# Attention with batch 1's value stage inside batch 0's value products, and whole fp32 operands for the first half of the queries

## The reference

```
V = x @ wv.T + bv                       # then out @ wo.T + bo: both fold into one 256 x 256 matrix here
pos = x @ w3d.T + b3d                   # three coordinates per token
dist = pairwise_l2(pos)
scores = where(causal, -inf, -dist[:, None] * scale)     # the same for all 16 heads
attn = softmax(scores)
x = x + attn @ V (projected)            # layer 1
x = x + experts(layernorm(x))           # layer 2: router, shared and routed experts
```

## Time and profile before

| What | Time, us |
|---|---|
| median of three runs | 684.58 |
| the profiled execution | 679.88 |
| its span | 678.1 |
| TensorE busy | 573.9 (85%) |
| VectorE busy | 449.8 (66%) |
| ScalarE busy | 339.8 (50%) |
| GpSimd busy | 211.7 (31%) |
| batch 0: first distance, first value product, last product's start | 62.01, 91.33, 142.21 |
| batch 1: first transpose, first distance, first value product, last product's start | 146.45, 188.05, 217.37, 268.25 |
| first TensorE work of the second layer | 277.94 |
| four tiles normalised on VectorE (L364) | 1.37 |
| two low parts of a transposed group (L370) | 1.28 |
| ScalarE's table load; exponential, high part of a block of 512 columns | 1.28; 0.62; 0.64 |

### The profile page before, as it was taken

One profiled execution on the slowest core, in us unless ns is written; L12 is line 12 of the kernel. 1 busy time (PEld: TensorE's weight loads), 2 busy tenths in 40 slices (PEclk: granted clock), 3 DMA queues, 4 the chain that ended last, 5 costly groups with the idle time before them and its releaser, 6 DMA issues.

```text
span 678.1 us, 11259 instructions
## 1 busy us (share of the span) xinstructions
PE 573.9 (85%) x3484; PEld 501.0 (74%) x3484; DVE 449.8 (66%) x1143; ACT 339.8 (50%) x710; POOL 211.7 (31%) x404
## 2 busy tenths in 40 slices
PE   3738989977498998684299899899999999998995
PEld 2727789977477998453278777688888888887884
DVE  4983898978578974878777776344444444444985
ACT  0416977614388781461454554255555555553331
POOL 2061120012323000000566777155455455452000
PEclk9978579979675999697599999899999999999998
DMA  9988000000000000920122222233333333325941
GB/s 283 313 246 3 1 1 1 2 0 1 1 0 1 2 1 1 347 118 1 55 79 87 91 91 86 79 102 102 109 105 102 106 103 106 104 79 177 383 161 62
DMA packets 57127, 62.59 MB, mean 92 GB/s; under 512 B 14736, under 2 KB 50448, under 8 KB 57072
## 3 DMA queue, kind: packets, MB, share of 16 engines
q1 hardware_dynamic: 49216, 43.46, 22.7%
q0 software_dynamic: 6480, 17.77, 7.3%
q10 hardware_dynamic: 1376, 0.66, 0.4%
HBM read 30.50 MB, written 31.37 MB: 91 GB/s over the span
## 4 chain that ended last, share of the span: by engine, by line
PE 42%; DVE 11%; ACT 4%; issue 3%; POOL 0%; DVEq 0%; ACTq 0%; POOLq 0%
PE bank L1208 12%; PE bank L1209 11%; PE bank L1210 11%; PE bank L1329 2%; PE bank L1345 2%; PE bank L1217 1%; DVE hf L1138 1%; ACT W_hi L911 1%; ACT h_hi L891 1%; DVE XN L974 1%; DVE XR L974 1%; DVE X L1129 1%; DVE XT_lo L1019 1%; DVE W_lo L1153 1%; DVE sw_lo L1027 1%
## 5 line engine op out<-in xcount | busy, mean ns | idle before, releaser
L843 POOL DMA_INDIRECT token_out<-YS,to_row x71 | 69.6, 980 | 96.1 <-ACT YS L941 92.5
L827 POOL DMA_INDIRECT slots_in<-XR,slot x64 | 69.8, 1091 | 82.5 <-DVE XR L1108 67.2
L575 PE MATMUL a_bank<-VO,E_hi 128*128 128x258 f32 x272 | 78.7, 289 | 4.3 <-DVE E_lo L482 4.3
L579 PE MATMUL a_bank<-VO,E_lo 128*128 128x258 f32 x272 | 78.1, 287 | 0.0
L577 PE MATMUL a_bank<-VO,E_hi 128*128 128x256 f32 x272 | 78.1, 287 | 0.0
L1179 DVE TENSOR_TENSOR hr<-bank,sr 128x256 f32<-128x256 f32 x71 | 30.1, 424 | 61.9 <-ACT sr L929 61.9
L453 DVE TENSOR_SCALAR E<-a_bank 128x512 f32<-128x512 f32 (+3 forms) x80 | 45.9, 606 | 29.3 <-PE a_bank L565 29.3
L1208 PE MATMUL bank<-W_hi,XST_hi 128*128 x142 | 62.4, 440 | 0.5 <-DVE XST_lo L1183 0.5
L1208 PE MATMUL bank<-XT_hi,sw_hi 128*128 128x512 f32 x128 | 52.4, 410 | 10.0 <-DVE XT_lo L1019 8.4
L929 ACT ACTIVATE sr<-bank 128x256 f32<-128x256 f32 x71 | 27.4, 385 | 64.1 <-PE bank L1210 64.1
L1210 PE MATMUL bank<-W_hi,XST_lo 128*128 x142 | 56.8, 400 | 0.0
(11 more groups left out here) (227 smaller groups left out, 1650.5 us busy)
## 6 DMA issues: line engine op xcount, KB each, us to landing
XS<-slots_in SPq DMA_DIRECT2D x71, 129.0 KB, 2.0
YG<-token_out SPq DMA_DIRECT2D x16, 512.0 KB, 7.8
slots_in<-blank SPq DMA_DIRECT2D x7, 1161.0 KB, 14.7
W_raw<-in_wT_dram SPq DMA_DIRECT2D x8, 768.0 KB, 12.6
X<-in_x_dram SPq DMA_DIRECT2D x8, 512.0 KB, 7.2
out_dram<-X SPq DMA_DIRECT2D x32, 128.0 KB, 2.1
token_out<-YS,to_row POOLq DMA_INDIRECT x71, 2.4
slots_in<-blank SPq DMA_DIRECT2D x1, 1032.0 KB, 13.7
```

Source lines behind the costliest of these rows:

```text
L575: pe.matmul(O_ps[Q % 2][j][:, 0:D + 2], E_hi[:, n % NE, cols], VO[:, kt, 0:D + 2], start=(kt == 0), stop=False)
L579: mm = pe.matmul(O_ps[Q % 2][j][:, 0:D + 2], E_lo[:, n % NE, cols], VO[:, kt, 0:D + 2], start=False, stop=(kt == qt))
L827: pool.indirect_dma_start(out=xs, out_offset=bass.IndirectOffsetOnAxis(ap=slot[k][:, t:t + 1], axis=0), in_=XR[:, t % 4, k, :], in_offset= ...
L843: pool.indirect_dma_start(out=ys, out_offset=bass.IndirectOffsetOnAxis(ap=to_row[:, i:i + 1], axis=0), in_=YS[:, i % NYS, :], in_offset=No ...
```

## The change

- **Whole operands in the first half.** Blocks 0 to 11 are no longer split. `VO` holds whole fp32 values and one column of ones (257 columns), and a tile pair is one fp32 product (L661 of the changed kernel). `VS` holds the values' high and low parts for the second half (L663 to L667).
- **The values are split on GpSimd** (L282, L284), per key tile behind its two selects.
- **Distances and products are interleaved.** 18 blocks of distances come first, then two more before each product until block 40 is reached.
- **Batch 1's stages 1 and 2 stand inside batch 0's products,** from product 17 on (`SIDE`), on all engines: group transposes, value tiles in pairs, maximum, features, feature transposes at products 34 to 36.
- Query groups share one set of four output banks; the other four serve distances and batch 1's value stage. `E_hi` and `E_lo` have four slots and lie where the first half's `E` was. In the second half ScalarE makes all high parts, VectorE the low ones two blocks ahead.
- All of batch 1's statistics run before batch 0's distances, and its root of the variance before batch 0's roots.

```diff
-VW = 2 * D + 2
+VW = D + 1
+HW = 2 * D + 2
-NE = 8
+NE = 4
-        O_ps = (bank[0:4], bank[4:8])
+        O_ps = bank[4:8]
+        N_FIRST = blocks.index((halves[1][0], 0))
+        EARLY = N_FIRST + 6
+        SIDE = 17
+        AHEAD = 2
+        def scores_before(n):
+
+            return range(min(EARLY + 2 * n, NBLK), min(EARLY + 2 * n + 2, NBLK))
...
@@ gpsimd, behind the two selects of key tile kt
+                    pool.wait_ge(s_voh, b * TB + kt + 1)
+                    pool.tensor_copy(VS[:, kt, 0:D], VO[:, kt, 0:D]).then_inc(s_vh, 1)
+                    pool.wait_ge(s_vh, b * TB + kt + 1)
+                    pool.tensor_tensor(VS[:, kt, D + 2:HW], VO[:, kt, 0:D], VS[:, kt, 0:D].bitcast(f32),
+                                       ALU.subtract).then_inc(s_vl, 1)
...
@@ scalar
+                roots(b, halves[0])
+                act.wait_ge(s_dist, b * NROW + GT * halves[0][-1] + GT)
+                for n in range(N_FIRST):
+                    exponential(b, n)
+                roots(b, halves[1])
+                act.wait_ge(s_dist, (b + 1) * NROW)
+                for n in range(N_FIRST, N_FIRST + 2 * AHEAD):
+                    exponential(b, n)
+                for n in range(N_FIRST, N_FIRST + AHEAD):
+                    high_part(b, n)
+                for n in range(N_FIRST, NBLK):
+                    if n + 2 * AHEAD < NBLK:
+                        exponential(b, n + 2 * AHEAD)
+                    if n + AHEAD < NBLK:
+                        high_part(b, n + AHEAD)
+                    if b + 1 < NB and n >= SIDE:
+                        next_values(b + 1, n - SIDE)
...
@@ vector
+            def next_values(b, m):
+                if m == 0:
+                    reciprocal_std(b)
+                if m % 2 == 0 and m // 2 < GB:
+                    normalise(b, m // 2)
+                if m % 2 == 1 and m // 2 < GB:
+                    group_lo(b, m // 2)
+                if 3 <= m < 3 + 2 * GB:
+                    for j in range(2):
+                        positions(b, (m - 3) // 2, (m - 3) % 2 * 2 + j)
+                if m == 2 * GB + 3:
+                    features(b)
...
+                for n, (Q, kt) in enumerate(blocks):
+                    for m in scores_before(n):
+                        square(b, m)
+                    if n == N_FIRST - 1:
+                        for m in range(N_FIRST, N_FIRST + AHEAD):
+                            split_lo(b, m)
+                    if N_FIRST <= n < NBLK - AHEAD:
+                        split_lo(b, n + AHEAD)
+                    if b + 1 < NB and n >= SIDE:
+                        next_values(b + 1, n - SIDE)
+                    if kt >= GT * Q:
+                        finish(b, Q, kt - GT * Q)
...
@@ tensor
+                    if whole:
+                        mm = pe.matmul(O_ps[j][:, 0:VW], blk[:, cols], VO[:, kt, :], start=(kt == 0), stop=(kt == qt))
...
+                for n in range(EARLY):
+                    distances(b, n)
+                for n in range(NBLK):
+                    for m in scores_before(n):
+                        distances(b, m)
+                    value_products(b, n)
+                    if b + 1 < NB and n >= SIDE:
+                        next_values(b + 1, n - SIDE)
```

More of the change, by code:

```diff
@@ L12 @@
 MW = D + 4
-VW = 2 * D + 2
-TRI = sum(S - P * k for k in range(TB))
+VW = D + 1
+HW = 2 * D + 2
 KR = 32
@@ new lines, in roots, with exponential @@
+            def roots(b, half):
+                for kt in range(GT * half[-1] + GT):
+                    row = row_of(half, kt)
+                    act.wait_ge(s_e2, b * NBLK + sq_blocks.index((half[-1], kt)) + 1 + NQ)
+                    act.wait_ge(s_diag, 2 * (b * TB + kt) + 2)
+                    act.activation(row, row, ACT.Sqrt).then_inc(s_dist, 1)
+            def exponential(b, n):
+                blk = block_of(*blocks[n])[0]
+                act.activation(blk, blk, ACT.Exp, scale=-SCALE).then_inc(s_exp, 1)
@@ new lines, in high_part @@
+            def high_part(b, n):
+                blk, _, w = block_of(*blocks[n])
+                act.wait_ge(s_exp, b * NBLK + n + 1)
+                act.wait_ge(s_eb, b * NBLK + free_for(n, HI_FREE) + 1)
+                act.activation(E_hi[:, n % NE, 0:w], blk, ACT.Copy).then_inc(s_eh, 1)
+            deviations(0)
+            group_hi(0, 0)
+            for g in range(GB):
+                if g + 1 < GB:
+                    group_hi(0, g + 1)
+                for j in range(GT):
+                    values(0, g, j)
@@ new lines, in _ @@
+            for n in range(3 * GB):
+                features(0, n)
+            for b in range(NB):
+                if b + 1 < NB:
+                    deviations(b + 1)
+                roots(b, halves[0])
[15 more added lines that the diff above has]
+                        next_values(b + 1, n - SIDE)
@@ L389, in _, with features @@
+            def features(b):
                 step = [0]
@@ new lines, in _ @@
+            reciprocal_std(0)
+            normalise(0, 0)
+            normalise(0, 1)
+            group_lo(0, 0)
+            for g in range(GB):
+                if g + 2 < GB:
+                    normalise(0, g + 2)
+                if g + 1 < GB:
+                    group_lo(0, g + 1)
+                for j in range(GT):
+                    positions(0, g, j)
+            features(0)
+            for t in range(TB + 1):
+                statistics(1, t)
+            for b in range(NB):
+                for n in range(EARLY):
+                    square(b, n)
+                for n, (Q, kt) in enumerate(blocks):
+                    for m in scores_before(n):
[9 more added lines that the diff above has]
+                        finish(b, Q, kt - GT * Q)
@@ new lines, in value_tile @@
+            def value_tile(b, g, j):
+                G = b * GB + g
+                pe.wait_ge(s_xtl, KC * G + 3 * KC)
+                pe.wait_ge(s_vol, GT * G + j + 1 + (2 if b else 0))
+                tok = slice(j * P, (j + 1) * P)
+                out = V_ps[b][j][:, 0:MW]
+                for c in range(KC):
+                    hi, lo = XT_hi[:, g % 2, c, tok], XT_lo[:, g % 2, c, tok]
+                    pe.matmul(out, hi, M_hi[:, c, :], start=(c == 0), stop=False)
+                    pe.matmul(out, hi, M_lo[:, c, :], start=False, stop=False)
+                    mm = pe.matmul(out, lo, M_hi[:, c, :], start=False, stop=(c == KC - 1))
+                mm.then_inc(s_vps[j % 2], 1)
@@ L543, in _, with turn_maximum @@
+            def turn_maximum(b):
                 pe.wait_ge(s_f, N_POS * b + 1)
@@ L567, in _ @@
[L567 to L583 removed]
+                if n >= 4:
+                    pe.wait_ge(s_fr, 3 * GB * b + n - 3)
```

386 lines of the change are left out of this document (179 added, 207 removed).

## The result

The changed kernel takes **702.67 us** (median of 4 runs, 700.14 to 708.89); the kernel before takes 684.99 beside it (4 runs, 682.52 to 685.44). The medians are 17.7 us apart; the ratio over the runs is 1.0283, 95% interval [1.0227, 1.0339]: slower. The forecast was +7.4 and 692.0, range 683 to 706. The sign, the order of the stretches and the three idle places came out as worked; one term, products 0 to 11, was far too small. One execution of the kernel with 22 blocks first, further down, took 1136.76 us in a slower state of the chip, and that kernel's numbers are those of its other five.

A forecast was written before the change was run, and what follows sets the result against it. TensorE was taken to set attention's end. Each batch ends 8.2 later from its first distance product, preparation gains 9.0 once: +7.4, giving 687.3 in the profile's terms, 692.0 on the runs' median; range 683 to 706.

The forecast's parts named there:

- The sign: Whole kernel: the change makes it slower, chance 0.69, against 0.11 for faster and 0.20 for within 0.5%.
- the three idle places: TensorE idle before the first line-661 matmul (at least 4), the first line-663 matmul (8.4) and product 31 (9.6).
- (a): From a batch's first distance product (D) to product 0, behind GpSimd's key tiles, roots and first exponential: 16.4 us.
- (b): Products 0 to 11 with 20 distance blocks: 16.3 + 7.7 = 24.0, plus 1.8 for low clock, 25.8 us.
- the clock stays low in (b): Rival: mixing distances with products keeps TensorE's clock low, +20 a batch, +47 in all, +15 in part; chance 0.12.
- (c): Second half's start: product 12 waits for late diagonals, root, table, exponentials, high and low parts; TensorE idle 8.4 us.
- (d): Second half's products from product 12: 35.8, low-clock start 1.8, waits for a finish 0.5, 38.1 us in sum.
- D to end: From a batch's first distance product to its last product: 88.7 us against 80.5, 8.2 later per batch.
- (e): Batch 1's preparation inside batch 0's products 17 to 36: 36.5 us against 45.5, 9.0 gained once.
- Cheap GpSimd: Rival: GpSimd's new operations run faster alone, 1.2 a key tile instead of 1.71, so kernel ends 7.6 faster; chance 0.14.
- The convoy: Rival: VectorE, ScalarE and TensorE delay each other exchanging tiles in batch 1's preparation, +15 us; chance 0.12.
- The features hide: Rival: batch 1's features take 5, the gap is 4, the sum is +1.5, no change; chance 0.10.

The follow-up runs named there:

- 22 blocks first: Late value splits, features in pieces, 22 distance blocks ahead of product 0 instead of 28, edited from the changed kernel: 671.99 us, ratio 0.9836.
- the first experiment: Changed kernel with GpSimd doing eight diagonals, then all 16 value splits, then the other eight diagonals: 691.16 us, ratio to before 1.0091.
- the second experiment: Changed kernel with all 40 distance blocks ahead of the first product instead of 18: 683.62 us, ratio to before 0.9985.
- The half-column run: Changed kernel with the first half's whole fp32 products over 129 of 257 columns, distances still interleaved: 714.06 us, ratio to before 1.0470.
- the first four experiments: Changed kernel with, separately: value splits moved, 691.16 us; all distances first, 683.62; batch 1's GpSimd shift after features, 698.87; features in pieces, begun earlier, 695.45.

## Why the prediction was right, and where it was off

**(a) D to product 0.** 16.4 forecast, 17.0 and 18.1 measured; the idle time 4, measured 4.3 and 4.0. The mechanism is shown by the first experiment: without the splits among the diagonals the wait is gone.

**(b) Products 0 to 11: the term that failed.** 25.8 forecast, 31.9 and 30.2 measured, 10.5 in sum, and most of what the forecast missed. The step that failed is 16.3 + 7.7 = 24.0: it adds products and distances as if each form stood alone, and puts the change from one to the other at nothing. The rows price the parts:

- *The products were right.* 0.43 a product instead of 0.45, so 36 take 15.5, not 16.3.
- *The change of form, missing from the sum.* A step of four products and two full blocks is 3.05; 4 x 0.43 and 4 x 0.23 are 2.65. The 0.40 left are the change there and back (95.85 to 96.19, for one, is 0.34 where 0.23 is usual). Ten such steps are 4.0 a batch.
- *The clock.* PEclk 0.86 over 32 and 0.92 over 30.3 is 4.5 and 2.4 lost, not 1.8.

15.5 + 7.7 + 4.0 + 4.5 = 31.7 in batch 0, and 29.6 with 2.4 in batch 1; 0.2 and 0.6 stay open. Two experiments bear the parts out. Where product 0 does not wait (the first) the stretch is 29.3 and 29.8 at PEclk 0.95 and 0.93, which is 1.5 and 2.1 of clock and 28.7 and 29.3 by the same sum. And 36 products without blocks between them (the second) take 18.24 at PEclk 0.87; less the clock's 2.4 that is 15.9, 0.44 each. So the rival "the clock stays low in (b)", which was given 0.12 and +15 to +47, came in small part. The half-column run shows that narrower products, in the same order with the same blocks, are kept at 1.2 GHz altogether.

**(c) Idle ahead of product 12.** 8.4 forecast, 7.9 twice. The chain was as described, diagonals 1.67 to 1.68 apart, root, table load, four exponentials. That it begins at the late distance blocks, and not at GpSimd alone, is shown by the second experiment (0.96 of wait with the same splits).

**(d)** 38.1 forecast; 39.6 in batch 1, with one wait of 0.89 for a finish and PEclk 0.94. D to end is 95.8 instead of 88.7, of which (b) 4.4, (a) 1.7, (d) 1.5, (c) -0.5.

**(e) Preparation inside the products.** Product 12 to the next D was to be 38.1 + 36.5 = 74.6; it is 75.5. The gap was forecast at 9.6 and is 8.8, and the features at 1.4 shorter: 9.6 long (165.11 to 174.74) against 11.6. The 3.4 of waits in the preparation are about 1.7 (0.99, 0.47, 0.25), the 1.5 of the maximum was not in the sum. So the preparation inside the products pays what was forecast, about 9, once.

**The sum.** D to D is 132.3, not 125.2 (+7.1), batch 1 +7.1, batch 0's D came 1.2 later: 15.4, which with the 7.4 gives 22.8, and attention's last product ends at 291.4 instead of near 268.5. The medians differ by 17.7. The other 5 are most likely the profiled execution of after and not the kernel. Against it, attention ends 16.3, 22.6, 7.9 and 13.5 earlier in the profiles of the first four experiments, whose medians are lower by only 11.5, 19.0, 3.8 and 7.2, and each of these profiled executions is within 2 of its kernel's median. In which stretch after's is long isn't shown. Before's profiled execution, 5.1 under its median, is short behind attention (400.2).

**The rivals.** Cheap GpSimd is refuted: 1.67 to 1.77 a key tile, above the 1.37 from which it would decide. The convoy didn't come. "The features hide" named the right lever: with the shift out of the way they take 5.3 and the gap is 4.5, as priced (5 and 4). But the change itself leaves the shift beside them.

**What the change is worth by its parts.** No run undid one half of it, so the split of the 17.7 is worked out, not measured: the preparation +9 gained once; the whole products, their GpSimd work and the order of the distances lose some 13 a batch, of which the products themselves are 36 x 0.07 = 2.5 by their rows. The order alone holds 19 of it while the splits stand among the diagonals, as the second experiment shows; the parts are not independent, since with the splits moved away 22 blocks first are as good as 28 or 34.

## What to carry to other kernels

Before a producer's work is put behind a consumer in an in-order queue, ask what the consumer waits for. Here 20 distance blocks stood behind a product that waits for an exponential, which waits for GpSimd: that cost 19 us, and a number in one line gave them back. With GpSimd's chain shortened, 16 blocks behind the product (22 first) cost nothing that could be measured. Price a mixture of matmul forms from a mixture: the change of form (0.40 a step) and a clock that stays low are in no row of either form alone. Take a product's price from the spacing of starts in two stretches of different length; a length divided by the count has the tail and the change of form in it. And where one engine prepares a thing in one long block between two hand-overs, cut it into pieces and start it early (7.2 gained here) before making it shorter (3.8).

## What the runs showed of the hardware

- Half of the columns made the kernel 11.4 us slower: TensorE without an idle moment for 36.6 us, at a granted clock of 0.50 throughout. The same narrow products by themselves had a mean of 0.76 over 11 us.
- A 257-column fp32 product, two matmuls in the trace, costs 0.43 at 2.4 GHz and 0.86 at 1.2 GHz; the three split matmuls of a pair are 0.36 at 2.4 GHz. Whole operands cost TensorE 0.07 a pair more.
- Going from such products to 64-row blocks and back costs 0.40 a step at 2.4 GHz, beyond the price of both.
- GpSimd's cast of 256 columns from fp32 to fp32r is 0.40, its subtraction 0.63 to 0.73.
- A 48-column VectorE operation with two inputs takes up to 0.78 beside a GpSimd addition and 0.20 alone, and the addition goes from 0.72 to 0.90 beside VectorE's 512-column low parts.
